# Chosen-token layer of an audio tower: gates picked once per unit, whole-unit gated rows, and the expert sum split around the narrowing products

## The reference, cut to what matters

```
def _L0_ffn_ref(x, Wg, W1, b1, W2, b2):
    k = min(max(int(l * C / e), 1), l)          # 187 of 748 tokens
    S = jax.nn.softmax(x @ Wg, axis=-1)
    St = jnp.swapaxes(S, 1, 2)
    G, I = jax.lax.top_k(St, k)
    ex = jnp.take_along_axis(x[:, None], I[..., None], axis=2)
    hmid = jax.nn.gelu(jnp.einsum('bekh,ehf->bekf', ex, W1) + b1[None, :, None, :], approximate=False)
    out = jnp.einsum('bekf,efh->bekh', hmid, W2) + b2[None, :, None, :]
    vals = G[..., None] * out
    new_x = jnp.zeros_like(x).at[jnp.arange(b)[:, None, None], I].add(vals)
    return new_x
```

## Time and profile before

| what | value |
|---|---|
| time, median of 3 runs | 2848.66 us |
| lowest, highest | 2844.8, 2848.93 us |
| the profiled execution | 2844.66 us |
| its span | 2842.9 us |
| busy, PE / PE weight load | 2453.6 / 1874.4 us |
| busy, DVE / ACT / POOL | 2100.0 / 1761.4 / 1060.1 us |
| 4 gate instructions of ACT, L1496, x256 | 109.6 us |
| 4 gate instructions of DVE, L1529, x256 | 83.5 us |
| gathers of POOL, L1383, x192 | 187.6 us |

### The profile page before, as it was taken

How to read it: one execution, slowest core, us unless ns; L and a number is a source line. 1 busy time by engine, 2 the same in 40 slices (tenths; PEclk the granted TensorE clock), 3 DMA queues, 4 the chain that set the end, 5 groups by cost and what they waited for, 6 DMA issues and landing times. The chain is left out here.

```text
span 2842.9 us, 53155 instructions
## 1 busy us (share of the span) xinstructions
PE 2453.6 (86%) x16811; PEld 1874.4 (66%) x16811; DVE 2100.0 (74%) x3869; ACT 1761.4 (62%) x3324; POOL 1060.1 (37%) x1210
## 2 busy tenths in 40 slices
PE   7979699999999997547888886888749997999993
PEld 7969454444444443436888885888637885888882
DVE  4545589999999994895888785677676664777775
ACT  3336177777777777425777773444437885777772
POOL 0025012222323233334444441333326775566664
PEclk9989699999999998758999997999979998999997
DMA  3109523333333330541111112300002111677748
GB/s 82 38 9 357 141 46 55 55 58 58 58 58 58 58 58 12 148 139 33 34 31 33 32 31 96 110 0 0 1 0 104 49 48 56 217 245 246 240 154 259
DMA packets 161301, 249.24 MB, mean 88 GB/s; under 512 B 41644, under 2 KB 106901, under 8 KB 154232
## 3 DMA queue, kind: packets, MB, share of 16 engines
q1 hardware_dynamic: 128888, 208.77, 27.2%
q0 software_dynamic: 19712, 38.13, 4.3%
q10 hardware_dynamic: 12544, 0.39, 0.2%
HBM read 155.24 MB, written 93.41 MB: 87 GB/s over the span
## 5 line engine op out<-in xcount | busy, mean ns | idle before, releaser
L1054 ACT ACTIVATE probs<-score 128x748 f32<-128x748 f32 (+1 forms) x768 | 568.3, 794 | 117.0 <-PE score L879 115.7
L983 DVE TENSOR_REDUCE part_max<-to_dve 128x1 f32<-128x512 f32 (+1 forms) x768 | 480.1, 684 | 83.4 <-PE to_dve L860 83.0
L2735 DVE TENSOR_TENSOR m_hid_lo<-m_hid,m_hid_hi 128x512 fp32r<-128x512 f32 x408 | 288.0, 707 | 158.5 <-ACT m_hid_hi L2708 158.5
L860 PE MATMUL to_dve<-k_stack,q_stack 48*128 48x512 f32 (+3 forms) x1536 | 351.5, 367 | 21.6 <-DMA k_stack<-k_parts 20.7
L879 PE MATMUL score<-q_stack,k_stack 49*128 49x374 f32 (+1 forms) x1536 | 317.4, 389 | 3.1 <-ACT probs L1054 1.0
L916 PE MATMUL o_sum<-probs,v_sb 128*17 128x374 f32 (+1 forms) x3072 | 315.6, 483 | 0.1
L879 PEld LDWEIGHTS score<-q_stack,k_stack 49*128 49x128 f32 (+1 forms) x1536 | 162.0, 181 | 225.0 <-ACT probs L1054 199.7
L1383 POOL DMA_INDIRECT f_row_in_c<-c_rows,c_ids x192 | 187.6, 977 | 258.9 <-DVE f_gated_c L1529 191.7
L860 PEld LDWEIGHTS to_dve<-k_stack,q_stack 48*128 48x128 f32 (+1 forms) x1536 | 223.0, 187 | 80.7 <-DVE part_max L983 36.7
L2631 POOL DMA_INDIRECT e_sums<-m_gated,m_row_in x216 | 212.5, 984 | 162.7 <-DVE m_gated L2753 101.8
L2708 ACT CAST m_hid_hi<-m_hid 128x512 fp32r<-128x512 f32 x408 | 248.3, 609 | 0.0
(11 more groups left out here) (449 smaller groups left out, 6158.3 us busy)
## 6 DMA issues: line engine op xcount, KB each, us to landing
m_weights<-e_records SPq DMA_DIRECT2D x54, 1028.0 KB, 6.6
q_stack<-q_parts SPq DMA_DIRECT2D x192, 93.5 KB, 3.1
k_stack<-k_parts SPq DMA_DIRECT2D x192, 93.5 KB, 4.2
e_slots<-blank SPq DMA_DIRECT2D x54, 260.0 KB, 3.7
m_row_in<-e_slots SPq DMA_DIRECT2D x54, 260.0 KB, 2.9
m_weights<-e_sums SPq DMA_DIRECT2D x16, 640.0 KB
e_records<-l_parts SPq DMA_DIRECT2D x16, 512.0 KB, 4.1
v_rows<-v_out SPq DMA_DIRECT2D x16, 408.0 KB, 6.0
```

The source lines that it names most:

```text
L860: last = pe.matmul(ring[i % RING][0:ROWS[c], at_col:at_col + keys.stop - keys.start], q_stack[its_slot][rows, j, c * P:c * P + ROWS[c]], k ...
L983: dve.tensor_reduce(part_max[0:ROWS[c], k, j, c, 0:1], ring[i % RING][0:ROWS[c], :], AX.X, ALU.max).then_inc(used, 1)
L1054: act.activation(probs[0:n, s % 2, m, 2 * j:2 * j + 2, :], score[tile][0:n, :, 0:HALF], ACT.Exp).then_inc(tile_used, 1)
L2735: dve.tensor_tensor(hid_lo[:, f % RING, :], hid[:, f % RING, :], hid_hi[:, f % RING, :].bitcast(F32), ALU.subtract).then_inc(lo_done, 1)
```

## The change

In `choose`, round r of the list reads only the columns from 8r on, at most 569 of them (8 + 748 - 187): the round's eight tokens cannot lie elsewhere.

In `chosen_ffn`:

- POOL picks each row's gate beforehand: two small `tensor_tensor` per unit make `gate` (`pick_gate`), between the gathers. The mask `owner` is set by eight memsets on DVE, and POOL waits for them before the first gather. A gather into the ring now waits for `turned` where it waited for `gated_n`.
- Gating is three instructions for the whole unit: DVE multiplies `back` by the gate, taken as a broadcast, into `weighed` (`weigh`); ACT rounds it (`round_gated`); DVE takes the rest (`split_gated`).
- `sums` is one tensor over three banks, so that `give_back` is four instructions (640 columns and 128, twice) for eight.
- PE's order: the first half of `combine(k-2)` stands between `widen(k)` and `narrow(k-1)`.
- DVE's order: `weigh`, one `mark`, `split_gated`, `mark`, `split_hid(k,0)`, `mark`, `split_x(k+1)`, `split_hid(k,1)`, `measure`. When a sequence has ended, `give_back` stands in the place of the first mark.

The core of the diff:

```
-                    then(dve.max(some, work[:, :]))
+                    window = work[:, 8 * r:min(T, 8 * r + 8 + T - k_tokens)]
+                    then(dve.max(some, window))
                     if r < SLOTS_E // 8 - 1:
-                        then(dve.match_replace(work[:, :], some, work[:, :], -1.0))
+                        then(dve.match_replace(window, some, window, -1.0))
...
-                for n in range(UNITS_C):
+                def gather(n):
                     if n >= RING:
-                        pool.wait_ge(gated_n, n - RING + 1)
+                        pool.wait_ge(turned, n - RING + 1)
...
+                def pick_gate(n):
+                    pool.wait_ge(gathered[n % RING], 16 * UNIT_TILES * (n // RING + 1))
+                    first = P + experts_of(n)[0]
+                    if n:
+                        pool.wait_ge(gate_made, n)
+                    pool.tensor_tensor(either[:, :, :], row_in[:, n % RING, :, first:first + 2], owner[:, :, :], ALU.mult
+                                       ).then_inc(picked, 1)
+                    if n >= 2:
+                        pool.wait_ge(weighed_n, n - 1)
+                    pool.wait_ge(picked, n + 1)
+                    pool.tensor_tensor(gate[:, n % 2, :], either[:, :, 0], either[:, :, 1], ALU.add).then_inc(gate_made, 1)
+
+                pool.wait_ge(owned, 2 * UNIT_TILES + 2)
+                for k in range(UNITS_C + PICK_BEHIND):
+                    if valid(k - PICK_BEHIND):
+                        pick_gate(k - PICK_BEHIND)
+                    if valid(k):
+                        gather(k)
...
                     if valid(k):
                         widen(k)
+                    if valid(k - 2):
+                        combine(k - 2, range(0, TILES // 2))
                     if valid(k - 1):
                         narrow(k - 1)
-                    if valid(k - 2):
-                        combine(k - 2, range(0, TILES // 2))
...
-                def gate_rows(n):
-                    act.wait_ge(turned_back, n + 1)
+                def round_gated(n):
+                    act.wait_ge(weighed_n, n + 1)
                     if n >= 2:
                         act.wait_ge(combined, n - 1)
-                    for part in gate_parts(n):
-                        at, tile, e = part
-                        act.activation(gated[at, n % 2, tile, 0, :], back[at, tile, :], ACT.Identity, bias=zero[at, :],
-                                       scale=gate_of(n, part)).then_inc(gate_hi, 1)
+                    act.copy(gated[:, n % 2, :, 0, :], weighed[:, n % 2, :, :]).then_inc(gate_hi, 1)
...
+                def weigh(n):
+                    dve.wait_ge(turned_back, n + 1)
+                    dve.wait_ge(gate_made, n + 1)
+                    if n >= 2:
+                        dve.wait_ge(gated_n, n - 1)
+                    dve.tensor_tensor(weighed[:, n % 2, :, :], back[:, :, :],
+                                      gate[:, n % 2, :].unsqueeze(2).broadcast_to([P, UNIT_TILES, P]), ALU.mult
+                                      ).then_inc(weighed_n, 1)
+
+                def split_gated(n):
+                    dve.wait_ge(gate_hi, n + 1)
+                    dve.tensor_tensor(gated[:, n % 2, :, 1, :], weighed[:, n % 2, :, :],
+                                      gated[:, n % 2, :, 0, :].bitcast(F32), ALU.subtract).then_inc(gated_n, 1)
...
-                        for c0, c1, n in PARTS_B:
+                        for c0, c1, n in [(0, TILES - 1, P), (TILES - 1, TILES, LAST)]:
                             h = g.h[0:n, b * TILES + c0:b * TILES + c1, :]
-                            last = dve.tensor_tensor(h, h, sums[c0 // 2][0:n, c0 % 2:c0 % 2 + c1 - c0, half, :], ALU.add)
+                            last = dve.tensor_tensor(h, h, flat[0:n, c0:c1, half, :], ALU.add)
...
                     if valid(k - 2):
-                        gate_rows(k - 2)
+                        weigh(k - 2)
                     if done is not None:
                         give_back(done // PER_BATCH)
-                    if valid(k - 1):
+                    elif valid(k - 1):
                         mark(k - 1, 0)
-                    if valid(k):
-                        split_hid(k, 0)
+                    if valid(k - 2):
+                        split_gated(k - 2)
+                    if done is not None and valid(k - 1):
+                        mark(k - 1, 0)
                     if valid(k - 1):
                         mark(k - 1, 1)
                     if valid(k):
-                        split_hid(k, 1)
+                        split_hid(k, 0)
                     if valid(k - 1):
                         mark(k - 1, 2)
                     if valid(k + 1):
                         split_x(k + 1)
+                    if valid(k):
+                        split_hid(k, 1)
```

More of the change, by code:

```diff
@@ L1345, in chosen_ffn @@
         marks = sb("f_marks", [P, 2, UNIT_TILES, T], F32R)
-        zero = sb("f_zero", [P, 1])
+        weighed = sb("f_weighed", [P, 2, UNIT_TILES, P])
+        either = sb("f_either", [P, UNIT_TILES, 2])
+        owner = sb("f_owner", [P, UNIT_TILES, 2])
+        gate = sb("f_gate", [P, 2, UNIT_TILES])
         turn = ps("f_turn", [P, 512])
@@ L1349, in chosen_ffn @@
         down, back = ps("f_down", [P, 512]), ps("f_back", [P, UNIT_TILES, P])
-        sums = [ps(f"f_sums{k}", [P, 2, 2, P]) for k in range(BANKS)]
-        (turned, rounded, split, up_done, gelu_done, hi_done, lo_done, down_done, kept, turned_back, gate_hi, gated_n,
-         marked, combined, half_added, added, zeroed) = (
+        sums = ps("f_sums", [P, BANKS, 2, 2, P])
+        (turned, rounded, split, up_done, gelu_done, hi_done, lo_done, down_done, kept, turned_back, weighed_n, gate_hi, gated_n,
+         marked, combined, half_added, added, owned, picked, gate_made) = (
             sem(s) for s in ("f_turned", "f_rounded", "f_split", "f_up_done", "f_gelu_done", "f_hi_done", "f_lo_done",
-                             "f_down_done", "f_kept", "f_turned_back", "f_gate_hi", "f_gated", "f_marked", "f_combined",
-                             "f_half_added", "f_added", "f_zeroed"))
+                             "f_down_done", "f_kept", "f_turned_back", "f_weighed_n", "f_gate_hi", "f_gated", "f_marked", "f_combined",
+                             "f_half_added", "f_added", "f_owned", "f_picked", "f_gate_made"))
         gathered = [sem(f"f_gathered{k}") for k in range(RING)]
-        GATES = 4
         def experts_of(n):
             return [2 * (n % PER_BATCH) + e for e in range(2)]
[L1363 to L1368, removed]
-            at, tile, e = part
-            return row_in[at, n % RING, tile, P + e:P + e + 1]
+        PICK_BEHIND = 3
         def valid(n):
@@ L1423, in turn_back @@
                     if n:
-                        pe.wait_ge(gated_n, n)
+                        pe.wait_ge(weighed_n, n)
                     for j in range(UNIT_TILES):
@@ L1432, in combine @@
                     pe.wait_ge(marked, UNIT_TILES * (n + 1))
+                    if i == 0 and b:
+                        pe.wait_ge(added, b)
                     for c in tiles:
-                        if i == 0 and b and c % 2 == 0:
-                            pe.wait_ge(added, BANKS * (b - 1) + c // 2 + 1)
                         for j in range(UNIT_TILES):
-                            last = pe.matmul(sums[c // 2][0:ROWS[c], c % 2, :, :], marks[:, n % 2, j, c * P:c * P + ROWS[c]],
+                            last = pe.matmul(sums[0:ROWS[c], c // 2, c % 2, :, :], marks[:, n % 2, j, c * P:c * P + ROWS[c]],
                                              gated[:, n % 2, j, :, :], start=(i == 0 and j == 0 and c % 2 == 0),
@@ L1542, in give_back @@
                     dve.wait_ge(combined, PER_BATCH * (b + 1))
-                    PARTS_B = [(0, 2, P), (2, 4, P), (4, 5, P), (5, 6, LAST)]
+                    flat = sums[:, :, :, :, :].rearrange("p k c h d -> p (k c) h d")
                     for half in range(2):
@@ L1546, in give_back @@
                             dve.wait_ge(half_added, b + 1)
-                        for c0, c1, n in PARTS_B:
+                        for c0, c1, n in [(0, TILES - 1, P), (TILES - 1, TILES, LAST)]:
                             h = g.h[0:n, b * TILES + c0:b * TILES + c1, :]
-                            last = dve.tensor_tensor(h, h, sums[c0 // 2][0:n, c0 % 2:c0 % 2 + c1 - c0, half, :], ALU.add)
[L1550 to L1553, removed]
+                            last = dve.tensor_tensor(h, h, flat[0:n, c0:c1, half, :], ALU.add)
+                        last.then_inc(added if half else half_added, 1)
                 def measure(b):
-                    dve.wait_ge(added, BANKS * (b + 1))
+                    dve.wait_ge(added, b + 1)
                     take_statistics(dve, g, b, range(TILES))
-                dve.memset(zero[:, :], 0.0).then_inc(zeroed, 1)
```

(3 more changed lines are left out.)

4 lines of the change are left out of this document (1 added, 3 removed).

## The result

The changed kernel takes 2910.16 us (median of 4 runs, 2907.41 to 2910.92) beside 2846.73 us for the kernel before: a ratio of 1.0221, with a 95% interval of 1.0204 to 1.0239. It is slower, as forecast, by 63 us where 50 were forecast. The profiled execution spans 2905.7 us for 2842.9.

The account below looks back on a forecast made before the run. DVE alone bounds the list rounds, two loops of about 6.3 us (gating, PE's) each unit; 2844.66 - 9 (lists) + 48.6 (sequences) + 0.5 (memsets) - 1.5 (tail) + 11 (clock) = 2894.3, stated as 2895 us, range 2866 to 2920.

Parts of the forecast that it names:

- The sign and the loop: 64 units of `chosen_ffn`: slower, as ACT's second `round_hid` and `round_x(k+1)` queue behind `keep`; 6.97 us a unit for 6.3.
- The walk: One mid-sequence unit followed through the new order by distances in the old trace: 6.97 us; a sequence 30.3 for 27.06.
- Rival A: Loop through ACT does not bind, shorter gating makes the kernel faster: 6.27 us a unit, 2823 us in all; chance 0.11.
- The end of a sequence: `give_back` in front of `split_gated` adds 1.25 us, `measure` in front of `weigh` adds 1.17 us.
- The list rounds: `choose`: 179 of 748 columns fall away, 0.19 to 0.20 us less in each of 47 DVE instructions, -9 us.
- The clock: PE at sequence ends and the unit behind: a third of some 29 longer waits bring a 1.2 us fall; +11 us net.
- rival B: Clock falls at nearly every end of a sequence: 29 x 1.2 = +35 us for +12, 2918 us; chance 0.09.
- POOL's wait for the memsets: Start of `chosen_ffn`: POOL waits for eight memsets before the first gather, +0.5 us.
- The gates: POOL's two instructions per unit for `pick_gate`: taken as 0, with some 3 us of POOL idle per unit as cover.
- Rival C: POOL late with the gates: each us beyond 3 us a unit costs 64 us, 2960 us with one; chance 0.03.
- The tail: Last unit of `chosen_ffn`: gating chain 1.7 us for 3.10 + 0.04, and a shorter give-back, -1.5 us.

Follow-up runs that it names:

- the ACT run: Changed kernel with ACT rounding the second half of the hidden rows before the bias step: 2901.62 us, ratio 1.0057 to the kernel before.
- the run with the sum behind: Changed kernel with PE's first half of the sum put back behind the narrowing products: 2813.95 us, ratio 0.9762 to the kernel before.
- The run with filled waits: Changed kernel with twelve unread products behind `widen` in the two long-wait steps of each sequence: 2919.03 us, ratio 1.0107 to the kernel before.
- their own run: Kernel before with only the list rounds' `window` of 569 columns: 2876.62 us, ratio 0.9974 to the kernel before.
- its second run: The changed kernel, unaltered, measured again on another chip: 2953.17 us, ratio 1.0226 to the kernel before.
- the first eight runs: Follow-up runs on two chips, where the kernel before took 2885.24 us (beside the first four) and 2890.51 us (beside the next four).
- the last two: Changed kernel with sum behind and statistics spread, 2765.61 us; the same with DVE's second `split_hid` ahead of statistics and `split_x`, 2771.64 us.

## Why the prediction was right, point by point

**The sign and the loop: right, shown.** The walk gave 6.97 us a unit, the profile 6.92. PE waits 0.49 and 0.46 where 0.5 and 0.4 were forecast, ACT 1.68 where 1.5 to 2, and has no idle time before `f_x_hi`; `weigh` takes 0.55 for 0.54. That ACT's queue behind `keep` closes the loop was argued then; the ACT run shows it (0.41 for 0.40), and the run with the sum behind shows that the moved products send the loop that way (6.92 to 5.51). Rival A is out: its condition, ACT not waiting at `f_made`, is met in no unit, although the gating did get shorter as it said.

**The end of a sequence: right.** 1.25 and 1.17 more were forecast, 1.32 and 1.16 are the undisturbed steps. An undisturbed sequence is 2 x 6.92 + 8.24 + 8.08 = 30.2 for 30.3; as it ran, with the falls, it is 32.0. The run with filled waits shows the undisturbed sequence all the way. Its 459.9 us beside 61 x 6.97 + 15 x 1.25 + 14 x 1.17 = 460.3 from the walk's own numbers look better than they are, by luck: the first of the 61 steps took 8.75 us at a low clock. Without that it is 458.0, and the walk is 0.5% long.

**The list rounds: right.** 8.7 us in the profile for 9, and 8.6, give or take 3 to 4, in their own run.

**The clock: the term that was mis-sized.** I took a third of 29 waits at 1.2 us, 12 us, and 20 fell at 1.38, 27.7. This 16 is more than the whole difference of 13 (63 for 50); the other terms together were 2 to 3 too high, the unit alone 61 x 0.05 = 3. The step that failed is the choice of a third, made from one fall among the waits of before, which I called 15 waits of 1.54 us. That was a misreading: 14 were of 1.54 with one fall, and the fifteenth was of 2.00 and had a fall too. This one row on a longer wait spoke for rival B, whose case "against" counted it as a wait that did nothing. It also makes two falls to take off, not one; what the second cost by itself is not separated. Of the new waits of 1.80 us 14 of 15 brought a fall, of those of 1.64 6 of 14. Rival B came true by two thirds, and its 2918 was nearer than the forecast. The measured time lies in the stated range since that range had been drawn to take B in.

**Small terms.** POOL's wait for the memsets costs nothing: the first one runs at the moment at which the block begins, and the first gather starts 0.7 us behind it, as it did before. The gates cost no wait either; POOL's 222.5 us for `f_weighed` are its own idle time. Rival C is out. The tail gained 0.8 for the 1.5 forecast.

## What to carry to other kernels

Before an instruction block is moved into an engine's idle time, look for who waits for what it pushes back, and what stands behind the waiting instruction in that engine's queue: nine products moved forward by one place cost 1.4 us a unit (6.92 for 5.51), since the next unit's rounding stood in ACT's line behind the step that reads what `narrow` makes. The whole change hides a part of that; beside the kernel before a unit is only 0.6 longer. Walking one period of the new order by start-to-start distances of the old trace gave the period to 1%. A wait of PE that grows can cost twice, once by itself and once by the slower clock behind it, 1.4 us a fall here; cut the longest ones, or give PE work in them. Look for every fall in the trace before with the wait in front of it, the last ones too.

## What the hardware showed that I had not expected

The granted clock reacts to waits of 2 us and less in a stretch that is otherwise busy. In the kernel before, 1 of 14 waits of 1.54 us had a fall, and the one of 2.00; in the changed kernel 6 of 14 of 1.64 (7 in its second run) and 14 of 15 of 1.80; of 29 filled with twelve unread products none. The wait's length is not all of it: with ACT's second rounding first, 8 of 15 of 1.80 had one. A fall costs 1.38 us of this path, 1.44 in the second run, and products that nothing reads brought the whole 34 us down.

POOL's addition of three columns takes 0.49 us by the profile, more than the product of six columns before it, 0.22 (medians of 64). The shortest addition takes 0.19, and POOL's spans are rough.

On the two chips of the first eight runs the mixture of experts, which none of these edits touch, lasts longer: 699 to 706 us in these eight runs, and 666 to 667 in the last two and in the first profiles of both kernels, from its first to its last `m_up` product. The chosen-token layer of the changed kernel differs by 4.5 us. The cause stays open.
